# Which tiles of the first pointwise convolution Vector takes, and which get their offset from TensorE

## The reference, cut to what matters

```python
def _fake_quant(x, bits):
    qmax = 2.0 ** (bits - 1) - 1.0
    scale = jnp.maximum(jnp.max(jnp.abs(x)) / qmax, 1e-08)
    y = x / scale
    yq = jnp.clip(y + jax.lax.stop_gradient(jnp.round(y) - y), -qmax - 1.0, qmax)
    return yq * scale
...
out = jax.nn.relu(_qconv(x, w1))                       # 32 -> 192 planes, 1x1: the stage of the change
out = jax.nn.relu(_qconv(out, w2, padding=1, groups=PLANES))   # depthwise 3x3
out = _qconv(out, w3)                                  # 192 -> 32 planes, 1x1
return out + x
```

## Time and profile before

| | |
|---|---|
| Median of 3 runs | 376.85 us (375.93 to 377.69) |
| The profiled execution's own time | 375.5 us |
| Its span, first to last instruction | 373.7 us |
| PE busy in the span | 355.8 us (95%) |
| DVE busy | 280.4 us (75%) |
| ACT busy | 234.7 us (63%) |
| Mean granted TensorE clock | 0.998 |

### The profile page before, as it was taken

One profiled execution on the slowest core, in us unless ns is written; L12 is line 12 of the kernel. 1 busy time (PEld: TensorE's weight loads), 2 busy tenths in 40 slices (PEclk: granted clock), 3 DMA queues, 4 the chain that ended last, 5 costly groups with the idle time before them and its releaser, 6 DMA issues.

```text
span 373.7 us, 7798 instructions
## 1 busy us (share of the span) xinstructions
PE 355.8 (95%) x2892; PEld 265.9 (71%) x2896; DVE 280.4 (75%) x529; ACT 234.7 (63%) x385; POOL 11.2 (3%) x15
## 2 busy tenths in 40 slices
PE   8989899999999999999999999999999898899984
PEld 7867877888697869687977888697867342466631
DVE  4857678847956894789379748946797799677986
ACT  5445849545953684287449545951886796277774
POOL 2000000120030000000000000000020000000000
PEclk9999999999999999999999999999999999999999
DMA  7847236224431533352335224132400000000006
GB/s 232 232 99 200 68 90 165 55 49 111 133 91 40 118 111 80 79 125 68 77 93 160 62 54 116 56 92 63 122 2 2 2 1 0 2 3 4 2 3 225
DMA packets 19630, 30.67 MB, mean 82 GB/s; under 512 B 4496, under 2 KB 11792, under 8 KB 19600
## 3 DMA queue, kind: packets, MB, share of 16 engines
q1 hardware_dynamic: 18960, 29.35, 29.7%
q10 hardware_dynamic: 640, 0.92, 1.1%
HBM read 10.86 MB, written 2.10 MB: 35 GB/s over the span
## 4 chain that ended last, share of the span: by engine, by line
PE 78%; DVE 7%; ACT 5%; DMA 4%; issue 3%; SPq 2%; ACTq 0%; DVEq 0%
PE sums_ps L787 25%; PE mix_ps L889 13%; PE ps L1468 9%; PE mix_ps L918 6%; PE sums_ps L845 5%; PE mix_ps L893 4%; PE mix_ps L845 4%; DMA D<-D 4%; PE ps L1427 3%; ACT q_I L1137 2%; PE ps L1410 2%; PE mix_ps L927 1%; DVE part L504 1%; PE mix_ps L829 1%; PE mix_ps L1031 1%
## 5 line engine op out<-in xcount | busy, mean ns | idle before, releaser
L787 PE MATMUL sums_ps<-D,w_hl 128*128 128x480 f32 (+1 forms) x504 | 118.1, 388 | 1.5 <-DMA D<-D 1.5
L787 PEld LDWEIGHTS sums_ps<-D,w_hl 128*128 128x128 f32 x504 | 93.2, 188 | 27.5 <-issue 5.9
L889 PE MATMUL mix_ps<-mix_hl,F_hl 128*128 128x288 f32 x360 | 64.3, 296 | 1.0 <-ACT Y L398 1.0
L398 ACT ACTIVATE Y<-mix_ps 128x288 f32<-128x288 f32 x120 | 49.0, 411 | 21.5 <-PE mix_ps L893 9.7
L889 PEld LDWEIGHTS mix_ps<-mix_hl,F_hl 128*128 128x128 f32 x360 | 55.3, 190 | 2.8 <-ACT Y L398 1.6
L336 ACT ACTIVATE r<-sums_ps,bias_sb 64x512 f32<-64x512 f32 x28 | 19.1, 683 | 42.1 <-PE sums_ps L787 41.9
L504 DVE TENSOR_TENSOR part<-mix_ps,part 64x512 f32<-64x512 f32 x16 | 11.1, 694 | 36.4 <-PE mix_ps L845 36.1
L893 PE MATMUL mix_ps<-mix_hl,X 96*128 96x288 f32 x120 | 35.2, 298 | 0.0
L1468 PE MATMUL ps<-q_q,diag 64*64 64x512 bf16 x576 | 33.4, 388 | 0.6 <-DVE q_q L1249 0.6
L1117 ACT ACTIVATE q_I<-ps,w_bias 128x1024 f32 x20 | 21.2, 1111 | 15.5 <-PE ps L1468 15.5
L356 ACT ACTIVATE D<-part 64x512 fp32r<-64x512 f32 x16 | 10.7, 668 | 31.6 <-DVE part L510 31.6
(11 more groups left out here) (147 smaller groups left out, 481.7 us busy)
## 6 DMA issues: line engine op xcount, KB each, us to landing
D<-D SPq DMA_DIRECT2D x88, 112.0 KB, 2.3
x_own<-in_x_pads SPq DMA_DIRECT2D x16, 256.0 KB, 3.3
F<-r SPq DMA_DIRECT2D x64, 64.0 KB, 2.0
F<-in_x_mix SPq DMA_DIRECT2D x16, 128.0 KB, 2.5
F<-part SPq DMA_DIRECT2D x32, 64.0 KB, 2.0
xb<-in_x_res SPq DMA_DIRECT2D x8, 256.0 KB, 2.9
out<-q_res SPq DMA_DIRECT2D x3, 512.0 KB, 2.8
w_raw<-in_w_conv SPq DMA_DIRECT2D x6, 192.0 KB, 3.9
```

Source lines behind the costliest of these rows:

```text
L398: nc.scalar.activation(Y[:, u, g], banks(p, u)[:, g % 4, 0:MIX], ACT.Copy).then_inc(y_out, 1)
L787: last = nc.tensor.matmul(tap_out(conv_sums(s, u)[:, bank, :], d), w_hl[:, wp, n, d, :], tap_in(D[f][u][:, xp], d), start=start and d == 1 ...
L889: nc.tensor.matmul(y, F_hl[u][:, xp, h, k], mix_hl[:, wp], start=n == 0, stop=False, skip_group_check=True)
```

## The change

Vector's six tiles are others, and with them Scalar's 18 and the pairs. Vector's list was 3, 7, 10, 13, 16, 20 and becomes 2, 5, 8, 11, 15, 19. Of Scalar's tiles, ten had their offset made by TensorE (0, 1, 2, 5, 8, 11, 14, 17, 19, 22) and six have it so afterwards (0, 1, 9, 14, 18, 22). In all, 16 tiles had offset products and 12 have them. The number of tiles for each engine, of folds and of closing steps stays.

```diff
 C1_TILES = NG * NB
-C1_DVE = [3, 7, 10, 13, 16, 20]
+C1_DVE = [2, 5, 8, 11, 15, 19]
 C1_ACT = [n for n in range(C1_TILES) if n not in C1_DVE]
 C1_PAIRS = list(zip(C1_ACT[0:-2:2], C1_ACT[1:-2:2]))
-C1_OFFSET = C1_DVE + [0, 1, 2, 5, 8, 11, 14, 17, 19, 22]
+C1_OFFSET = C1_DVE + [0, 1, 9, 14, 18, 22]
 C1_AHEAD = [0, 1, 2]
```

## The result

The changed kernel takes 374.53 us (median of 9 runs, 373.32 to 375.12) against 376.87 (9 runs, 375.7 to 378.46) for the kernel before: a ratio of 0.9935, 95% interval 0.9917 to 0.9953, or 2.3 us. I had said 376.1, within 375.0 to 377.4, so the time lies outside the range. The profiled execution took 373.52 us, its span 371.7 us.

The account below looks back on a forecast made before the run. Bound: when Vector begins the stage's closing maxima. Head start 0.87 less 0.19 for an added fold wait gave 0.68; stepped closing 315.70 - 315.01 = 0.69 us, 0.7 off the median: 376.15, say 376.1, range 375.0 to 377.4.

Parts of the forecast that it names:

- The bound: End of the 24-tile stage: Vector's start of the closing maxima counts, 315.10 and 315.70 before; clock stays at 1.00.
- The first tile: Vector's first tile becomes tile 2 and begins at 298.00 in place of 298.87, a head start of 0.87 us.
- The price of a free slot: TensorE's first product for a new tile starts 0.17 us after Scalar's read of the slot ends.
- Steps at 0.05: Tile-by-tile timing of the three engines with a free slot priced at 0.05 us; forecast gain 0.9 us.
- tile 5: Vector's second tile in the new order: forecast to start at 299.91, after Vector idles 0.77 us for TensorE.
- the closing: Vector's closing maxima at the stage's end: forecast to begin at 314.41 and 315.01.
- My case of 0.5 to 0.8 us: Main forecast for the stage: Vector's end comes 0.5 to 0.8 us earlier, central value 0.69; chance 0.60.
- the head start arrives whole: Rival on Vector's earlier first tile: stalled TensorE restarts sooner than 0.17, gain 0.9 to 1.0 us, time 375.9; chance 0.17.
- Who gains: In the stage: Vector's head start of 0.87 us brings the gain; fewer offsets, 0.25 us alone, add nothing to it.
- Folds 4 and 5: Two Vector folds in a row ahead of tile 19: forecast to stand 1.33 us apart.
- Scalar: Scalar's last read in the stage: forecast to end at 314.57, not late, margin falling from 0.75 to 0.44 us.
- The range: Whole-kernel time around 376.1: 0.3 for larger gain, 0.7 for none, some 0.8 of run spread; 375.0 to 377.4 us.

## Why the prediction was wrong

**The bound, right.** The end of the stage hung on Vector's closing maxima, before and after, and the clock stayed at 1.00 in the stage, though TensorE's products now waited for the slots of six tiles. The Trainium skill, TensorE: Matmul & The Clock Gate, section "A second HAM failure mode: psum-queue depth-cycling", says that short moments of idling while PSUM banks are cycled through can send the clock back and forth. That did not show here.

**The first tile, right.** Forecast at 298.0; the stage begins 1.04 sooner here, so 296.95 is 297.99 on the old scale.

**The price of a free slot, wrong in size.** This is the term of the sum that failed. I took 0.17 us from a row where the products were not waiting, only keeping their pace; the five waits on Scalar in the changed kernel show 0.04 to 0.06. Steps at 0.05 give 0.93 us, and 0.93 is what the stage gave. On the old scale tile 5 came at 299.81 and not 299.91, tile 15 at 306.76 and not 307.00, the closing at 314.17 and not 314.41. This term turned 0.93 into 0.69. My case of 0.5 to 0.8 us, with 0.60 of the chances, did not come; the rival above it did, with 0.17, and by its own condition: Vector's waits shrank to 0.68 before tile 5 and 0.10 before tile 15, where it had said 0.63 and 0.1. Its name, "the head start arrives whole", doesn't fit, for half of the head start was lost in front of tile 5.

**Who gains, wrong in part.** I wrote that the head start is the gain and that fewer offsets add nothing to it. Without the head start 0.54 of 0.93 remain, so the first half is wrong. Alone, the fewer offsets give 0.32, and the new tiles, with ten offsets in one placement, -0.05; for that placement the second half is wrong too, and for others it stays open. The steps came within 0.05 us of all of these when I put the lists in; I had run them for one part only and reasoned the other.

**Folds 4 and 5, right.** They stand 1.33 us apart (306.87 and 308.19).

**Scalar, right in kind.** Its last read ends 19.31 behind the quantising instruction, 314.50 on the old scale, against 314.57. Its margin ahead of the second closing maximum fell from 0.75 to 0.28 (313.46 against 313.74), and not to the 0.44 forecast, since that maximum came sooner by more.

**The range, wrong.** For the time of the whole, the step that failed is the last: "around these some 0.8 of the runs' own spread", from three runs, laid about a median of three. The 0.24 us that the slot's price cost is too little to explain it: 376.1 less 0.24 is 375.86, well inside 375.0 to 377.4, and 374.53 lies outside. The profiles say the same: a span of 373.0 was forecast and 371.7 measured, and of these 1.3 us 1.04 arose in the dense block and 0.24 in the stage. The same kernel before had medians of 376.85, 376.87, 375.47, 375.66, 375.4, 375.62 and 375.95 over the measurements of this study, the first two of which share runs. The changed kernel had 374.53, then 375.05, 375.57 and 375.15; the last three lie in the range. A hit there would have been luck, as the range stood about a median 0.9 to 1.5 us above the later ones of the same kernel. The profiles place the variation in the dense block: two kinds of executions 1.5 us apart, in shares that differ from one measurement to the next, and late transfers. In the nine runs of the first measurement of the changed kernel, six were of the faster kind; in the three later measurements 12 of 36. The nine of the kernel before that they stand against average 377.13, which is above even the slower kind's 376.58; their clocks are not in the result, so how many were of which kind can't be told. So: 0.92 us of the 2.3 is shown to be the change's; the other 1.4 is shown not to repeat, and its cause stays open.

## What to carry to other kernels

When several engines feed each other through a few slots, list every tile's start for all of them with the prices of the trace, and put each part of the change through the same list alone: here neither part alone was worth what both were together. When a part can be done in more than one way, such as the choice of ten tiles here, one way doesn't speak for the others. A single instance of a wait is a poor price for it; check first that the engine wasn't simply keeping its own pace. And before a forecast of less than a microsecond is set against a measured ratio, cut the profile at the last instruction that the change can't touch: the stage's time repeated to 0.01 us while its start moved by 2.9.

## What the runs showed of the hardware

A read-out by Scalar with a bias took 1.12 to 1.18 us on average in the seventeen profiles and 1.02 to 1.07 without; what counts in a row of them is the distance from start to start, about 1.00 and 0.92. TensorE's first product for a slot that Scalar had just read began 0.04 to 0.06 us behind the end of the read, in five waits of the changed kernel. A fold on Vector that had to wait for Scalar and for the fold before it, both ending within 0.03 us of each other, started 0.46 us behind the later one, in both executions; one with the wait for Scalar alone started 0.03 behind. At one place of the dense block TensorE's clock fell to its lower level behind a wait of 1.81 to 2.43 us in nine profiles of fourteen. It stayed up in the other five, with a first wait of 0.62 to 1.68, in one of them with a wait of 1.82 nine products later. With five small products in that wait, the mean clock was 0.996 or more in all but one of 36 executions.
